# Recurrent layer and first attention: where the norm statistics, the low-rank product's mixing and the group root are computed

## The chip, the cores and the metric

The kernel runs on one core of a Trainium2 chip, in one launch. The metric is the device time in microseconds, the median of several runs.

## The reference

Input x is (16, 64, 256): 1024 rows of 256 channels, with a context of the same shape. Four layers follow one another: (0) self attention, cross attention (16 heads of 16) and an MLP; (1) an instance-normed attention with 64x64 weights; (2) two cross attentions with 16 heads of 128 and an MLP; (3) a recurrent layer with a channel MLP. The change touches layer 0's attentions and layer 3. Layer 3, cut to what matters:

```
xa = ln(x, ln1_w, ln1_b)
sx = concat([state[:, 1:2] - xa[:, :1], xa[:, :-1] - xa[:, 1:]], axis=1)
xxx = tanh((xa + sx * maa_x) @ maa_w1).reshape(b, l, 5, 32)
xxx = einsum('blfd,fde->blfe', xxx, maa_w2)
xm = xa[:, :, None] + sx[:, :, None] * (maa_stack + xxx)     # xk, xw, xv, xr, xg
w = exp(-exp(time_decay + tanh(xw @ td_w1) @ td_w2))
r, k, v, g = xr @ Wr.T, xk @ Wk.T, xv @ Wv.T, silu(xg @ Wg.T)
# scan over the 64 steps, 32 heads of 8: s = k v^T + w * s;  out = r (u * k v^T + s)
og = group_norm(out, groups of 8) * gn_w + gn_b
x1 = x + og * g @ Wo.T
xc = ln(x1, ln2_w, ln2_b); sx2 = shifted difference of xc
return x1 + sigmoid((xc + sx2 * ffn_maa_r) @ Wfr.T) * (relu((xc + sx2 * ffn_maa_k) @ Wfk.T) ** 2 @ Wfv.T)
```

## The kernel before

The 1024 rows are 8 tiles of 128 rows (two sequences of 64). Each engine has its program written out by hand, and semaphores join them: `done[name].did(i)` is raised by the step `name` of tile i, `done[name].at(i)` is waited for. Every engine executes its steps in the written order, so a step that waits holds up all behind it.

**First attention** (`attn0_*`). 16 items (self for tiles 0 to 7, cross for tiles 0 to 7, interleaved) run through 19 slots. A step called as `step(slot - 2)` works on the item that entered two slots earlier. VectorE (`attn0_vector`) computes per slot: the row statistics of a finished cross item (`row_stats`, `row_variance`: only in slots 9, 11 and 13 to 18), the mask product (`multiplied`, L590), its addition (`masked`, L596), `top`, the context (`context`, L614 and L618), `shifted` (L606), `stats` and `variance` of the next item (L538 to L548), `keys` (L572, which spreads the keys over a block diagonal, kdiag), and `add` (L626). TensorE's `scores` (L345) waits for kdiag. ScalarE evacuates, takes the exponential and makes the normed rows (`normed`, L204) from the scale that GpSimd computes (`rstd`, L196 and L198). GpSimd also adds the bias rows and splits the finished rows in a high and a low part (`row_split`, L219 and L221) for the MLP behind it; the MLP's first products and gelus (L811, L838) are begun in the last attention slot.

**Recurrent layer** (`rwkv_*`). The 8 tiles run through 16 slots of the same kind. TensorE's slot of tile i has `turn` (transposes), `lora` (the first low-rank product, into mx_ps), `mixes` (the second, L1871); one slot later `decay1`, `project` (r, k, v, g), `spread0`; two later `decay2`, `spread1`; three later `gather`, `center`, `turn_heads`, `attended`; four later `turn_ffn`; five later `ffn1`, `ffn2`. The transposed normed rows lie in `xa` with one column of state ahead of each sequence. The low-rank product of xa + sx * maa_x is taken without that sum: as xa (shifted by one column) times w1 - w1 * maa_x plus xa times w1 * maa_x, both weights prepared by GpSimd in `rwkv_consts_gpsimd` while layer 2 runs. That makes 12 matmuls, 24 TensorE instructions in 4-byte floats.

VectorE's slot holds `products0`, `bonus`, `out_heads`, `mix2` (L2211), `products1` (L2227), `group_sum` (L2278), `shift` (L2193, makes sx), the first three scans (`scan0`, L2246), `group_rstd` (L2284), `group_norm` (L2291), the other five scans (`scan1`, L2246), `ffn` (L2305), `receive` (L2262), `gate`, `attended` (L2297), `close` and `mix1` (L2203). ScalarE squares the centred heads, and `std` (L2082) takes the root of the group variance with the Sqrt function, whose table is another than that of the Tanh before and after it (L2111). GpSimd's slot holds the norm scales, copies of state columns, `receive` (L2391, the product rs0 over the first three scans), `gated` (L2398) and `bonus` (L2405). TensorE's `turn_ffn` of tile i waits for VectorE's `ffn` of tile i - 1.

Slots are counted by TensorE's below: in slot s it does `turn(s)`, the first scans of tile s - 2, the group norm of tile s - 3 and the ffn product of tile s - 5. Slot 3 is the first with a group norm, slot 5 the first with an ffn product.

Of the kernel before, what the change touches and what calls it, by code (L numbers as in the profile page):

```python
# [19 lines left out]
P = 128  # L20
# [247 lines left out]
def attn0_tensor(pe, ph, m):  # L268
# [139 lines left out]
    for slot in range(SLOTS):  # L408
# [12 lines left out]
        turn_rows(slot - 3)  # L421
# [6 lines left out]
def attn0_scalar(act, ph, m):  # L428
# [85 lines left out]
    for slot in range(SLOTS):  # L514
# [3 lines left out]
        rows(slot)  # L518
        if slot == SLOTS - 1:
            for u in range(STREAMS):  # L520
                gelu_rows(act, ph, m, ACT.Gelu_apprx_tanh, u, 0, 0)
        mlp_rows(slot - 3)
# [6 lines left out]
def attn0_vector(vec, m):  # L529
# [109 lines left out]
    for slot in range(SLOTS):  # L639
# [14 lines left out]
        if slot:  # L654
            stats(slot + 1)
            variance(slot + 1)
        keys(slot)
        if slot == 0:
            vec.wait_ge(m.s_x[1], 16)
            stats(1)  # L660
            variance(1)
# [3 lines left out]
def attn0_gpsimd(pool, ph, m):  # L665
# [34 lines left out]
    for slot in range(SLOTS + 1):  # L700
        if slot == 0:
            rstd(0)
        row_rstd(slot - 3)
        bias(slot)
        row_bias(slot - 4)
        row_split(slot - 4)
# [1104 lines left out]
def rwkv_consts_gpsimd(pool, m, before):  # L1811
# [5 lines left out]
    pool.tensor_tensor(m.maa_w1s, m.maa_w1[:, :, :], wide("maa_x", NX), ALU.mult)  # L1817
# [4 lines left out]
    pool.tensor_tensor(m.maa_w1[:, :, :], m.maa_w1[:, :, :], m.maa_w1s, ALU.subtract)  # L1822
# [4 lines left out]
def rwkv_tensor(pe, m, before):  # L1827
# [21 lines left out]
    def lora(i):  # L1849
        xa = m.xa[i % 2]  # L1850
        pe.wait_ge(*done["xa"].at(i))
        pe.wait_ge(*done["a_state"].at(i))
        if i >= 1:
            pe.wait_ge(*done["mixed"].at(i - 1))
        for n, width in enumerate((P, P, 2 * DM)):
            cols = slice(n * P, n * P + width)
            last = product(m.mx_ps[0:width, n * P:(n + 1) * P],
                           [(m.maa_w1[:, k, cols], xa[:, k, :, 1:S + 1]) for k in range(KD)]
                           + [(m.maa_w1s[:, k, cols], xa[:, k, :, 0:S]) for k in range(KD)])
# [154 lines left out]
def rwkv_scalar(act, m):  # L2014
# [64 lines left out]
    @of_tile  # L2079
    def std(i):  # L2080
        act.wait_ge(*done["gsum"].at(i))
        act.activation(m.sm[0][:, :], m.sm[0][:, :], ACT.Sqrt, bias=m.col("eps"), scale=1.0 / HS)\  # L2082
            .then_inc(*done["gstd"].did(i))

    @of_tile
# [47 lines left out]
    act.wait_ge(m.s_gn, 1)  # L2133
    a_normed(0)
    for slot in range(TILE_SLOTS):
# [5 lines left out]
        ffn_rows(slot - 5)  # L2141
        rows(slot)
# [3 lines left out]
        std(slot - 3)  # L2146
# [6 lines left out]
def rwkv_vector(vec, m, ph):  # L2153
    done = m.tile_done

    def stats(i, tag, at):
        a = i % 2
        vec.bn_stats(m.stats[a][:, at, :], m.x[:, i, :]).then_inc(*m.own_vec.did(tag + "_stats", i))

    def variance(i, tag, at):  # L2160
        a = i % 2
        vec.wait_ge(*m.own_vec.at(tag + "_stats", i))
        if i >= 2:
            vec.wait_ge(*done[tag + "_xn"].at(i - 2))
        vec.bn_aggr(m.mv[a][:, at, :], m.stats[a][:, at, :]).then_inc(*m.own_vec.did(tag + "_mv", i))
        vec.wait_ge(*m.own_vec.at(tag + "_mv", i))
        vec.tensor_scalar(m.rstd[a][:, at:at + 1], m.mv[a][:, at, 1:2], EPS, None, ALU.add)\
            .then_inc(*done[tag + "_eps"].did(i))

    @of_tile  # L2170
    def a_stats(i):
        vec.wait_ge(m.s_acc, 14 + 2 * (i // 4))
        stats(i, "a", 0)

    @of_tile
    def a_variance(i):
        variance(i, "a", 0)

    @of_tile
    def f_stats(i):  # L2180
        vec.wait_ge(*done["x1"].at(i))
        stats(i, "f", 1)

    @of_tile
    def f_variance(i):
        variance(i, "f", 1)

    @of_tile
    def shift(i):
# [4 lines left out]
            .then_inc(*m.own_vec.did("sx", i))  # L2194

# [625 lines left out]
```

## Time and profile before

| | us |
|---|---|
| median of 3 runs | 1036.51 |
| lowest, highest | 1035.86, 1045.05 |
| profiled execution, its own time | 1037.27 |
| its span | 1035.4 |
| TensorE busy | 946.3 (91%) |
| VectorE busy | 595.9 (58%) |
| ScalarE busy | 431.0 (42%) |
| GpSimd busy | 410.0 (40%) |
| first attention | about 0 to 165 |
| recurrent layer | about 838 to 1035.4 |

PE is TensorE's matmul queue, PEld its weight loads, DVE VectorE, ACT ScalarE, POOL GpSimd. A row of the timeline has the start, the duration, the engine, the source line, the operation, output and inputs with their shapes, how many instructions are merged, and in brackets how long the engine was idle before it and what ended that. A row of a table by line has the count, then busy us in all, mean ns of one, and the idle time before them.

### The profile page before, as it was taken

The numbers are of one execution on the slowest core, as the hardware profiler recorded it, in microseconds if no ns is written. First come the engines' busy times: TensorE is split into PE (matmuls) and PEld (weight loads), VectorE is DVE, ScalarE is ACT, GpSimd is POOL, SyncE is SP. The second block draws the span as 40 slices with busy tenths as digits, with TensorE's granted clock in tenths as the row PEclk, the third lists the DMA queues.
The fourth block names the chain that finished last, engine by engine and source line by source line (L and its number), as shares of the span: only waits on it lengthen the run. The fifth ranks groups of instructions, "written<-read, shape, count | busy, mean of one in ns | idle before, by whom it ended". The sixth has DMA issues, their size and how long they took to land.

```text
span 1035.4 us, 21403 instructions
## 1 busy us (share of the span) xinstructions
PE 946.3 (91%) x8296; PEld 803.9 (78%) x8296; DVE 595.9 (58%) x1004; ACT 431.0 (42%) x910; POOL 410.0 (40%) x558
## 2 busy tenths in 40 slices
PE   6888887968989999999999999999996978999986
PEld 4667765856778888899887988888985877878854
DVE  5889993667644443334363444433357457988871
ACT  3566663237643333333343333333323223545542
POOL 2223253875366343333166432433317512333320
PEclk9999997999999999999998999999998998999997
DMA  9000000140011110111101111110100100000000
GB/s 307 11 2 1 3 1 11 42 150 1 2 52 47 51 51 24 47 36 51 47 19 54 37 51 46 51 51 21 41 16 22 41 1 1 1 6 7 6 12 15
DMA packets 24145, 37.12 MB, mean 36 GB/s; under 512 B 4432, under 2 KB 16528, under 8 KB 23824
## 3 DMA queue, kind: packets, MB, share of 16 engines
q1 hardware_dynamic: 24080, 36.23, 11.3%
q8 instruction: 44, 0.72, 0.3%
q14 instruction: 21, 0.17, 0.1%
HBM read 35.17 MB, written 1.05 MB: 35 GB/s over the span
## 4 chain that ended last, share of the span: by engine, by line
PE 76%; DVE 8%; ACT 7%; issue 4%; POOL 4%; DMA 1%; SPq 0%; ACTq 0%; POOLq 0%; DVEq 0%
PE ps L1193 16%; PE ps L722 11%; PE ps L1832 9%; PE ps L1210 9%; PE ps L1252 6%; PE ps L1228 3%; PE ps L811 3%; PE ps L394 2%; PE ps L345 2%; PE ps L1238 2%; PE ps L1983 1%; PE ps L1910 1%; PE ps L297 1%; ACT sb L1617 1%; PE ps L1871 1%
## 5 line engine op out<-in xcount | busy, mean ns | idle before, releaser
L772 POOL TENSOR_TENSOR sb<-sb 128x256 fp32r<-128x256 f32 (+1 forms) x128 | 95.5, 746 | 302.0 <-DMA sb<-in_heads_a 149.7
L1193 PE MATMUL ps<-sb 128*128 128x512 f32 x768 | 187.8, 396 | 1.0 <-issue 1.0
L1193 PEld LDWEIGHTS ps<-sb 128*128 128x128 f32 x768 | 139.6, 188 | 33.0 <-ACT sb L1318 3.2
L722 PE MATMUL ps<-sb 128*128 128x256 f32 x1152 | 148.7, 287 | 0.5 <-DVE sb L859 0.4
L722 PEld LDWEIGHTS ps<-sb 128*128 128x128 f32 x1152 | 142.5, 193 | 2.7 <-issue 0.8
L774 POOL TENSOR_TENSOR sb<-sb 128x256 fp32r<-128x256 f32 (+1 forms) x128 | 115.6, 903 | 10.0
L1832 PE MATMUL ps<-sb 128*128 128x128 f32 (+2 forms) x672 | 101.0, 309 | 12.4 <-ACT sb L2116 6.3
L1832 PEld LDWEIGHTS ps<-sb 128*128 128x128 f32 (+1 forms) x672 | 89.6, 202 | 21.8 <-issue 8.0
L1415 DVE SCALAR_TENSOR_TENSOR sb<-ps,sb 128x512 fp32r<-128x512 f32 x64 | 45.1, 747 | 97.5 <-ACT sb L1351 97.5
L1210 PE MATMUL ps<-sb 128*128 128x256 f32 x768 | 99.2, 285 | 0.4 <-DVE sb L1383 0.4
L1210 PEld LDWEIGHTS ps<-sb 128*128 128x128 f32 x768 | 95.0, 191 | 3.0 <-issue 0.9
L1395 DVE TENSOR_REDUCE sb<-ps 128x8 f32<-128x520 f32 x32 | 22.4, 699 | 127.9 <-PE ps L1228 127.9
L1318 ACT ACTIVATE sb<-ps,sb 128x512 f32<-128x512 f32 x64 | 43.8, 685 | 109.2 <-PE ps L1193 109.2
L196 POOL TENSOR_TENSOR sb<-sb 128x1 f32<-128x1 f32 x40 | 22.0, 550 | 146.4 <-DVE sb L548 72.9
L1351 ACT ACTIVATE sb<-ps,sb 128x512 fp32r<-128x512 f32 x64 | 40.5, 684 | 82.3 <-PE ps L1252 82.3
L1252 PEld LDWEIGHTS ps<-sb 64*128 64x128 f32 x1024 | 61.3, 192 | 9.2 <-issue 5.1
L1252 PE MATMUL ps<-sb 64*128 64x64 f32 x1024 | 65.8, 280 | 1.6 <-ACT sb L1344 1.6
L1383 DVE TENSOR_TENSOR sb<-ps,sb 128x512 f32<-128x512 f32 x64 | 43.9, 690 | 37.4 <-PE ps L1210 37.1
L811 PE MATMUL ps<-sb 128*128 128x512 f32 x192 | 51.3, 427 | 8.1 <-POOL sb L774 4.6
L811 PEld LDWEIGHTS ps<-sb 128*128 128x128 f32 x192 | 39.0, 208 | 17.7 <-POOL sb L774 5.8
L1335 ACT ACTIVATE sb<-ps,sb 128x512 f32<-128x512 f32 x64 | 43.4, 679 | 15.7 <-PE ps L1193 15.5
L838 ACT ACTIVATE sb<-ps,sb 128x512 f32<-128x512 f32 x32 | 21.9, 689 | 66.3 <-PE ps L811 66.2
(211 smaller groups left out, 1595.7 us busy)
## 6 DMA issues: line engine op xcount, KB each, us to landing
sb<-in_heads_a SPq DMA_DIRECT2D x32, 386.0 KB, 3.0
sb<-in_heads_c SPq DMA_DIRECT2D x16, 256.0 KB, 3.6
sb<-in_heads_b SPq DMA_DIRECT2D x32, 128.0 KB, 2.9
sb<-in_mlp_a SPq DMA_DIRECT2D x16, 128.5 KB, 2.1
sb<-in_mlp_b SPq DMA_DIRECT2D x16, 128.0 KB, 2.1
sb<-in_w_r SPq DMA_DIRECT2D x1, 2048.0 KB, 7.6
sb<-in_encT SPq DMA_DIRECT2D x1, 1024.0 KB, 5.9
sb<-in_ctx SPq DMA_DIRECT2D x1, 1024.0 KB, 8.3
```

What stands on the lines that cost most here:

```text
L722: last = pe.matmul(m.acc(t), lhsT[x], rhs[w], start=opens and n == 0, stop=False, skip_group_check=True)
L772: pool.tensor_tensor(high, src, one, ALU.mult).then_inc(*G.did(name + "_high", u))
L774: pool.tensor_tensor(low, src, high.bitcast(F32), ALU.subtract).then_inc(*G.did(name, u))
L811: last = pe.matmul(m.ps[u][:, c, :], m.w_parts[u][w][:, k * P:(k + 1) * P], m.h_parts[x][:, k, c * 512:(c + 1) * 512], start=n == k == 0, ...
L1193: last = pe.matmul(m.ps[u][:, c, :], m.w_parts[u][w][:, (KD * q + k) * P:(KD * q + k + 1) * P], rows[x][:, k, c * 512:(c + 1) * 512], star ...
L1210: last = pe.matmul(m.ps[u0][:, c0, b * 2 * P:(b + 1) * 2 * P], m.enc_parts[x][:, k, (2 * j + b) * P:(2 * j + b + 1) * P], m.wv_parts[w][:, ...
L1252: last = pe.matmul(m.ps[1 - u][:, o, j * P + b * S:j * P + (b + 1) * S], m.v[j // 2][half, 2 * (j % 2) + b, u, :], m.pT[u][half, j, b * S: ...
L1318: act.activation(head_keys_of(m, u)[:, 8 * c:8 * c + 8, 0:S], m.ps[u][:, c, :].rearrange("p (n k) -> p n k", k=S), ACT.Identity, bias=m.he ...
L1335: act.activation(m.qT[u][:, c * 512:(c + 1) * 512], m.ps[u][:, c, :], ACT.Identity, bias=m.head_col(u, 0)).then_inc(*hd.qk.act.did(f"q{c}" ...
L1383: vec.tensor_tensor(dst, m.ps[u0][:, c0, :].rearrange("p (b c) -> p b c", b=2), bc(m.v_row[:, :], 1, [P, 2, 2 * P]), ALU.add).then_inc(*hd ...
L1415: vec.scalar_tensor_tensor(out=m.ctx_low(u, o), in0=m.ctx_ps(u, o), scalar=m.bv[u][:, :], in1=m.ctx_high(u, o).bitcast(F32), op0=ALU.add, ...
L1832: last = pe.matmul(out, lhsT, rhs, start=n == 0, stop=n == len(terms) - 1)
```

## The change

In the recurrent layer: (1) VectorE computes `xl` = xa + sx * maa_x in a new step `lora_rows` (two operations) behind `shift`, and TensorE's `lora` takes that alone, with half as many matmuls; the two scaled weights aren't prepared. (2) The statistics of both layer norms go from VectorE's bn_stats to ScalarE: a sum by Identity, the negated mean, a sum of squares by Square; GpSimd finishes variance, root and scaled mean. `a_rstd` moves one GpSimd slot on. (3) The group norm's root goes from ScalarE's Sqrt and VectorE's reciprocal to GpSimd, as power -0.5 over 128x32, in a new step `group_rstd` ahead of `receive`.

In the first attention: (4) VectorE's `stats` and `variance` of the next item come behind `keys`; GpSimd's `row_split` comes ahead of `row_rstd` and `bias`; in the last slot TensorE turns the last rows between the two first MLP products, and ScalarE evacuates them ahead of the gelus.

```diff
@@ -418,7 +418,10 @@
             for u, free in enumerate((done["qT"], done["pT1"])):
                 pe.wait_ge(*free.at(len(ITEMS) - 1))
                 fc1(pe, ph, m, 4, u, 0, 0)
-        turn_rows(slot - 3)
+                if u == 0:
+                    turn_rows(slot - 3)
+        if slot < SLOTS - 1:
+            turn_rows(slot - 3)
         keys(slot)
         turn_context(slot - 2)
         query(slot)
@@ -516,10 +519,10 @@
+        mlp_rows(slot - 3)
-        mlp_rows(slot - 3)
@@ -651,14 +654,11 @@
         top(slot - 1)
         context(slot - 2)
         shifted(slot - 1)
-        if slot:
-            stats(slot + 1)
-            variance(slot + 1)
         keys(slot)
         if slot == 0:
             vec.wait_ge(m.s_x[1], 16)
-            stats(1)
-            variance(1)
+        stats(slot + 1)
+        variance(slot + 1)
         add(slot - 2)
 
 
@@ -700,10 +700,10 @@
+        row_split(slot - 4)
-        row_split(slot - 4)
@@ -1814,12 +1814,10 @@
-    pool.tensor_tensor(m.maa_w1s, m.maa_w1[:, :, :], wide("maa_x", NX), ALU.mult)
-    pool.tensor_tensor(m.maa_w1[:, :, :], m.maa_w1[:, :, :], m.maa_w1s, ALU.subtract)
@@ -1847,16 +1845,13 @@
-        xa = m.xa[i % 2]
-        pe.wait_ge(*done["xa"].at(i))
-        pe.wait_ge(*done["a_state"].at(i))
+        pe.wait_ge(*m.own_vec.at("xl", i))
-                           [(m.maa_w1[:, k, cols], xa[:, k, :, 1:S + 1]) for k in range(KD)]
-                           + [(m.maa_w1s[:, k, cols], xa[:, k, :, 0:S]) for k in range(KD)])
+                           [(m.maa_w1[:, k, cols], m.xl[i % 2][:, k, :]) for k in range(KD)])
@@ -2077,12 +2072,6 @@
-    def std(i):
-        act.wait_ge(*done["gsum"].at(i))
-        act.activation(m.sm[0][:, :], m.sm[0][:, :], ACT.Sqrt, bias=m.col("eps"), scale=1.0 / HS)\
-            .then_inc(*done["gstd"].did(i))
-    @of_tile
@@ -2115,11 +2104,33 @@
+    def stats(i, tag, at, dst):
+        a, own = i % 2, m.own_act
+        total, squares, mean = m.mv[a][:, at, 0:1], m.mv[a][:, at, 1:2], m.rstd[a][:, at:at + 1]
+        if i >= 2:
+            act.wait_ge(*done[tag + "_turned"].at(i - 2))
+        act.activation(dst[a][:, :], m.x[:, i, :], ACT.Identity, accum_out=total).then_inc(*own.did(tag + "_sum", i))
+        act.wait_ge(*own.at(tag + "_sum", i))
+        act.activation(mean, total, ACT.Copy, scale=-1.0 / D).then_inc(*own.did(tag + "_mean", i))
+        act.wait_ge(*own.at(tag + "_mean", i))
+        act.activation(dst[a][:, :], m.x[:, i, :], ACT.Square, bias=mean, accum_out=squares)\
+            .then_inc(*done[tag + "_eps"].did(i))
+    @of_tile
+    def a_stats(i):
+        act.wait_ge(m.s_acc, 14 + 2 * (i // 4))
+        stats(i, "a", 0, m.xn)
+    @of_tile
+    def f_stats(i):
+        act.wait_ge(*done["x1"].at(i))
+        stats(i, "f", 1, m.xn_last)
-        if i >= 2:
-            act.wait_ge(*done[tag + "_turned"].at(i - 2))
@@ -2139,11 +2151,12 @@
         lora(slot - 1)
         decay1(slot - 2)
         ffn_rows(slot - 5)
+        f_stats(slot - 4)
+        a_stats(slot + 1)
         rows(slot)
         decay2(slot - 2)
         f_normed(slot - 4)
         square(slot - 3)
-        std(slot - 3)
         relu(slot - 5)
         receive(slot - 5)
         relu_square(slot - 5)
@@ -2152,38 +2165,6 @@
-    def stats(i, tag, at):
-        a = i % 2
-        vec.bn_stats(m.stats[a][:, at, :], m.x[:, i, :]).then_inc(*m.own_vec.did(tag + "_stats", i))
...
@@ -2192,6 +2173,18 @@
+    @of_tile
+    def lora_rows(i):
+        vec.wait_ge(*m.own_vec.at("sx", i))
+        if i >= 2:
+            vec.wait_ge(*done["lora"].at(i - 2))
+        for k in range(KD):
+            split = lambda x: x.rearrange("p (b s) -> p b s", b=2)
+            last = vec.scalar_tensor_tensor(out=split(m.xl[i % 2][:, k, :]), in0=split(m.sx[i % 2][:, k * P:(k + 1) * P]),
+                                            scalar=m.col("maa_x", k), in1=m.xa[i % 2][:, k, :, 1:S + 1], op0=ALU.mult,
+                                            op1=ALU.add)
+        last.then_inc(*m.own_vec.did("xl", i))
@@ -2275,19 +2268,16 @@
+        if i >= 1:
+            vec.wait_ge(*done["gstd"].at(i - 1))
-    @of_tile
-    def group_rstd(i):
-        vec.wait_ge(*done["gstd"].at(i))
-        vec.reciprocal(m.rc[0][:, :], m.sm[0][:, :]).then_inc(*m.own_vec.did("grstd", i))
-        vec.wait_ge(*m.own_vec.at("grstd", i))
+        vec.wait_ge(*done["gstd"].at(i))
@@ -2321,27 +2311,23 @@
-        f_variance(slot - 7)
+        lora_rows(slot - 3)
-        group_rstd(slot - 6)
-        a_stats(slot)
-        a_variance(slot)
-        f_stats(slot - 6)
@@ -2350,8 +2336,15 @@
+        a, own = i % 2, m.own_pool
+        var, squares, mean, scale = (m.mv[a][:, at, 0:1], m.mv[a][:, at, 1:2], m.rstd[a][:, at:at + 1],
+                                     m.rstd2[a][:, at:at + 1])
-        norm_scales(pool, m, i % 2, at, (tag + "_pow", i), done[tag + "_rstd"].did(i))
+        pool.tensor_scalar(var, squares, 1.0 / D, EPS, ALU.mult, ALU.add).then_inc(*own.did(tag + "_var", i))
+        pool.wait_ge(*own.at(tag + "_var", i))
+        pool.tensor_tensor(scale, var, m.col("pow"), ALU.pow).then_inc(*own.did(tag + "_pow", i))
+        pool.wait_ge(*own.at(tag + "_pow", i))
+        pool.tensor_tensor(mean, mean, scale, ALU.mult).then_inc(*done[tag + "_rstd"].did(i))
@@ -2383,6 +2376,18 @@
+    @of_tile
+    def group_rstd(i):
+        n = D // HS
+        pool.wait_ge(*done["gsum"].at(i))
+        pool.tensor_scalar(m.sm[0][:, :], m.sm[0][:, :], 1.0 / HS, EPS, ALU.mult, ALU.add)\
+            .then_inc(*m.own_pool.did("group_var", i))
+        pool.wait_ge(*m.own_pool.at("group_var", i))
+        if i >= 1:
+            pool.wait_ge(*done["normed"].at(i - 1))
+        pool.tensor_tensor(m.rc[0][:, :], m.sm[0][:, :], m.col("pow").to_broadcast([P, n]), ALU.pow)\
+            .then_inc(*done["gstd"].did(i))
@@ -2410,8 +2415,9 @@
     for slot in range(TILE_SLOTS):
         f_rstd(slot - 6)
         a_state(slot - 2)
-        a_rstd(slot)
+        a_rstd(slot - 1)
         first(slot - 4)
+        group_rstd(slot - 5)
         receive(slot - 4)
         f_state(slot - 6)
         gated(slot - 5)
@@ -2538,8 +2544,9 @@
+        m.xl = [scaled(at, P) for at in (KD * (2 * D + P), KD * (2 * D + 2 * P))]
```

## Rows read from the trace of the kernel before

**Rows 1.** windows, recurrent layer: length, busy us by engine, PEclk, DMA share

```profile
899.00:969.00 70.00, 70.00 (x598) 57.89 (x597) 61.12 (x97) 37.45 (x81) 26.42 (x30) 1.00 0.02 5
...
881.00:886.00 5.00, 5.00 (x32) 5.00 (x32) 4.97 (x9) 1.40 (x3) 1.81 (x1) 0.66 0.00 0
```

**Rows 2.** chain of waits, one full slot: start, us, what

```profile
942.12 3.67 PE ps L1832 x28
...
946.15 1.45 PE ps L1832 x8
```

**Rows 3.** timeline of VectorE, slot 6 from its mix1 to the next

```profile
929.09 1.49 DVE L2203 TENSOR_TENSOR sb<-ps,sb 128x1280 f32<-128x1280 f32 x1 [0.90 <-PE ps L1871]
...
935.22 0.42 DVE L2278 TENSOR_REDUCE sb<-sb 128x32 f32<-128x256 f32 x1
...
935.89 1.85 DVE L2246 TENSOR_TENSOR_SCAN sb<-sb 128x256 f32<-128x256 f32 x3
...
938.01 0.42 DVE L2291 TENSOR_TENSOR sb<-ps,sb 128x256 f32<-128x256 f32 x1
...
938.36 4.16 DVE L2246 TENSOR_TENSOR_SCAN sb<-sb 128x256 f32<-128x256 f32 x5
...
943.02 0.42 DVE L2305 SCALAR_TENSOR_TENSOR sb<-sb,ps 128x256 f32<-128x256 f32 x1 [0.51 <-PE ps L1832]
...
949.17 1.49 DVE L2203 TENSOR_TENSOR sb<-ps,sb 128x1280 f32<-128x1280 f32 x1 [0.90 <-PE ps L1871]
```

**Rows 4.** timeline, first attention, slots 12 and 11

```profile
104.90 1.23 DVE L590 TENSOR_TENSOR sb<-ps,sb 128x1024 f32<-128x1024 f32 x1
...
110.54 0.42 DVE L538 BATCH_NORM_STATS2 sb<-sb 128x6 f32<-128x256 f32 x1
...
112.80 1.09 PE L345 MATMUL ps<-sb 64*64 64x256 f32 x16 [0.72 <-issue]
...
113.95 1.23 DVE L590 TENSOR_TENSOR sb<-ps,sb 128x1024 f32<-128x1024 f32 x1 [0.92 <-PE ps L345]
```

**Rows 5.** groups by line, ScalarE

```profile
L2111 ACT ACT_TABLE_LOAD x6 | 7.7, 1283 | 0.1
...
L1617 ACT ACTIVATION_READ_ACCUMULATOR sb<-ps,sb 128x1 f32 x32 | 6.9, 217 | 0.0
```

**Rows 6.** groups by line, power on GpSimd by columns, VectorE's reciprocal

```profile
L196 POOL TENSOR_TENSOR sb<-sb 128x1 f32<-128x1 f32 x40 | 22.0, 550 | 146.4 <-DVE sb L548 72.9 <-DVE sb L2167 50.7 <-DVE sb L563 21.9
...
L962 POOL TENSOR_TENSOR sb<-sb 128x4 f32<-128x4 f32 x4 | 4.1, 1034 | 11.4 <-DVE sb L911 11.4
...
L1487 POOL TENSOR_TENSOR sb<-sb 128x8 f32<-128x8 f32 x1 | 1.7, 1655 | 0.0
...
L2284 DVE RECIPROCAL sb<-sb 128x32 f32<-128x32 f32 x8 | 2.6, 329 | 1.2 <-ACT sb L2082 1.2
```

**Rows 7.** timeline, GpSimd beside VectorE

```profile
236.63 1.22 POOL L1759 TENSOR_SCALAR sb<-sb 128x256 f32<-128x256 f32 x1
...
237.37 1.22 DVE L1693 TENSOR_TENSOR sb<-sb 128x1024 f32<-128x1024 f32 x1
...
901.72 4.63 DVE L2246 TENSOR_TENSOR_SCAN sb<-sb 128x256 f32<-128x256 f32 x5
...
937.82 1.81 POOL L2391 TENSOR_TENSOR sb<-sb 128x768 f32<-128x768 f32 x1 [3.23 <-DVE sb L2246]
...
938.36 1.83 DVE L2246 TENSOR_TENSOR_SCAN sb<-sb 128x256 f32<-128x256 f32 x1
```

**Rows 8.** timeline, mix1 of slots 3 and 4, ffn product of slot 9

```profile
892.45 1.49 DVE L2203 TENSOR_TENSOR sb<-ps,sb 128x1280 f32<-128x1280 f32 x1 [1.08 <-PE ps L1871]
...
909.41 1.47 DVE L2203 TENSOR_TENSOR sb<-ps,sb 128x1280 f32<-128x1280 f32 x1
...
998.23 0.42 DVE L2305 SCALAR_TENSOR_TENSOR sb<-sb,ps 128x256 f32<-128x256 f32 x1 [0.24 <-PE ps L1832]
```

**Rows 9.** timeline, TensorE at the first attention's end

```profile
172.67 5.49 PE L811 MATMUL ps<-sb 128*128 128x512 f32 x12 [3.46 <-POOL sb L221]
```

More of the change, by code:

```diff
@@ L2133, in rwkv_scalar @@
     act.wait_ge(m.s_gn, 1)
+    a_stats(0)
     a_normed(0)
@@ L2154, in rwkv_vector @@
     done = m.tile_done
-    def stats(i, tag, at):
-        a = i % 2
-        vec.bn_stats(m.stats[a][:, at, :], m.x[:, i, :]).then_inc(*m.own_vec.did(tag + "_stats", i))
[L2160 to L2168, printed above, removed]
-    @of_tile
[L2171 to L2186, printed above, removed]
     @of_tile
@@ L2277, in group_sum @@
         vec.wait_ge(*done["square"].at(i))
+        if i >= 1:
+            vec.wait_ge(*done["gstd"].at(i - 1))
         vec.tensor_reduce(m.sm[0][:, :], m.sq[:, :].rearrange("p (h j) -> p h j", j=HS), AX, ALU.add)\
             .then_inc(*done["gsum"].did(i))
-    @of_tile
-    def group_rstd(i):
-        vec.wait_ge(*done["gstd"].at(i))
-        vec.reciprocal(m.rc[0][:, :], m.sm[0][:, :]).then_inc(*m.own_vec.did("grstd", i))
     @of_tile
@@ L2540, in build @@
         scaled = lambda at, n: consts[:, at:at + KD * n].rearrange("p (k n) -> p k n", k=KD)
-        m.maa_w1s, m.wfks, m.wfrs, m.headsum_u = (
-            scaled(at, n) for at, n in ((0, NX), (KD * NX, D), (KD * (NX + D), D), (KD * (NX + 2 * D), P)))
+        m.wfks, m.wfrs, m.headsum_u = (
+            scaled(at, n) for at, n in ((0, D), (KD * D, D), (KD * 2 * D, P)))
+        m.xl = [scaled(at, P) for at in (KD * (2 * D + P), KD * (2 * D + 2 * P))]
         m.xa = [x[:, 0:4 * (S + 1)].rearrange("p (k b s) -> p k b s", k=KD, b=2) for x in m.wa]
```

## Prediction, made before the change was built

> **What bounds the kernel now.** I read the windows first. The recurrent layer takes the last 197 us of the span. In its middle TensorE is busy for all of 70 us at full clock, VectorE for 61 of them; in the filling before it the granted clock of one stretch of 5 us was 0.66 after gaps of nearly 1 us [rows 1]. Then the chain of waits of one full slot: it is TensorE instruction behind instruction, with no gap [rows 2], and the slot lasts 949.17 - 929.09 = 20.08 us [rows 3]. So in slots 5 to 7 TensorE's own order is the limit. VectorE is the next one: it waits only 0.90 us before mix1 and 0.51 before the ffn product [rows 3]. Before slot 5 and after slot 7 the chain goes to and fro between TensorE, VectorE and ScalarE. In the first attention TensorE stands 0.72 us ahead of the scores (the page has "issue", but kdiag ends just before it), and VectorE stands 0.92 us before the product with the mask in slots that have no row statistics, and not at all in those that have them [rows 4].
>
> **Part 1, the low-rank product.** TensorE's x28 is 24 instructions of the lora product and 4 twice as wide, so 3.67/32 = 0.115 us for a narrow one [rows 2]. Twelve of 24 go: 1.4 us in each of 8 slots. VectorE gets two products of 128x128 a slot; from the shortest neighbour rows I take 0.55 us together. They are issued before the first scans. TensorE's lora now waits for them, but comes 7 us after shift in a full slot, so that wait costs nothing there.
>
> **Part 2, statistics to ScalarE.** VectorE loses bn_stats, bn_aggr and one small operation (about 0.75 us) for f in each slot, and for a in slots up to 4. ScalarE gets an Identity and a Square over 256 columns, each with an accumulator read (217 ns, [rows 5]), and a one-column copy: I estimate 1.45 us with its waits, twice in a slot with both. Its idle time before the row evacuation is over 3.5 us in a full slot, so it is covered. If that cover were gone, turn and lora would come late by the rest. At the start it is not: the chain to the first normed row grows by about 0.9 us, a_stats(1) stands in front of the first row evacuation (0.85 us), VectorE's shift and product (1.05 us) come before a product that is 1.5 us shorter: +1.3 us. GpSimd's operations for the scale are all one column wide, 0.25 and 0.55 us each, and it has idle time for them.
>
> **Part 3, the root of the group norm on GpSimd.** This is the large term. Out go a Sqrt on ScalarE with two table loads of 1.28 us around it [rows 5] and a reciprocal of 0.33 us on VectorE. In comes a pow over 128x32 on GpSimd. The kernel has pow over 1, 4 and 8 columns: 550, 1034 and 1655 ns [rows 6]. That is 155 ns a column from 4 to 8, and 161 from 1 to 4. For 32 columns I get 1655 + 24 x 155 = 5.4 us. The lower bound is VectorE's whole operation on such a tile, 0.33 us [rows 6]; the value lies near the three rows of the same operation, which fall on a line. Behind it are queued on GpSimd the product rs0, gated and bonus; and on VectorE group_norm waits, with the second part of the scans (five of them), the ffn product, the receiving product and gate behind it.
>
> Times from the start of group_sum (935.22 in the slot shown): before, group_norm starts at 2.79 and the last scan ends at 7.30 [rows 3]. After: 0.42 for the sum, 0.1 for the semaphore, 0.3 for the variance, up to 0.3 that it waits behind shift, 0.1, 5.4 for the pow, 0.1: group_norm starts at 6.8. The first scan behind it is held up by GpSimd's rs0 product, as now: a scan of 0.66 takes 1.83 us while that product of 1.81 us runs [rows 3, 7]. It starts 0.05 us after the pow and holds that scan until 8.45, and the five scans end at 11.45. Now gated and bonus fall into the scans as well. Where gated fell there, the five took 4.63 and not 4.16 us [rows 7, 3], so 0.48 for each: 12.4, which is 5.1 us later than now.
>
> What that costs in a slot:
> - Slots 3 and 4 have no ffn; VectorE decides. Receive, gate, attended follow the scans, 2.0 us, and mix1 starts at 6.04 + 12.4 + 2.1 = 20.5 us after the mix1 before; slot 4 took 909.41 - 892.45 = 16.96 [rows 8]. That is +3.6, and in slot 3, with a little more slack and an easier start, +2.5.
> - Slots 5 to 7: the ffn product ends at 6.04 + 12.4 + 0.45 = 18.9, and turn_ffn, attended, decay1 and mixes need 3.4 more on TensorE: 22.3 against 20.08, and against 19.68 in slot 5: +2.6, +2.2, +2.2.
> - Slots 8 and 9: the ffn product starts when the scans end. It started at 998.23 in slot 9 [rows 8], with group_sum at 991.05; now 11.6 behind that: +4.4, and +4.7 in slot 8 the same way.
> - Slot 10 has no scans: turn_heads waits for the pow and delays the ffn product: +1.6.
> These are 23.8 us. What the shorter lora still gives is in the slots before a group norm exists: slots 1 and 2, 1.8 us each, since TensorE ran at half clock in a part of them; with +1.3 at the start the filling gives -2.3. In slots 3 to 7 the 1.4 us is counted already: TensorE just waits longer. Recurrent layer: +21.5.
>
> **Part 4, first attention.** kdiag moves 0.74 us up [rows 4], since the statistics start 0.74 before it. In the nine slots without row statistics the scores come 0.55 to 0.75 us earlier. Their cost: the normed row comes 1.3 us later, so GpSimd's bias addition now meets VectorE's masking (two tiles from SBUF) and holds it up by some 0.4. I take 0.3 for each, -2.7. In row slots VectorE has no gap, and order does not change its sum: 0. In the last slot, the rows are turned and evacuated ahead of the table load and both gelus, and GpSimd's split, for which TensorE waits 3.46 us [rows 9], comes 2 us earlier: -2. Moving row_split up uses idle GpSimd time: 0. Together -5 (between -2 and -8). The two products that leave the weights' preparation lie under a TensorE that is busy throughout: 0.
>
> **Sum.** +21.5 - 5 = +16.5. The profiled execution took 1037.3 us (span 1035.4); 1053.8 from there, and the median of the runs shown is 0.8 lower: **1053 us**.
>
> **A rule that would make it worse.** A scan that starts beside GpSimd's product waits for nearly all of it [rows 7]. But a VectorE product of two SBUF tiles that started at 237.37, beside a GpSimd operation with 0.48 us to go, took its usual 1.22 us [rows 7]: GpSimd holds VectorE only as long as it still reads, and reads well ahead. A pow of 32 columns is little to read and much to compute, so I count it as not holding the scans. The Trainium skill (SBUF — State Buffer, Who interferes with whom) says the opposite in the general case: whoever of GpSimd and a VectorE operation with two SBUF inputs comes first gets the shared ports for its whole instruction. The row at 237.37 speaks against that as far as it goes.
>
> **Rivals.**
> - *The pow holds the ports.* Then lora's second product and the first scans wait for the pow and run behind it: 1.75 us more in slots 3 to 7 and 1.2 in 8 and 9, +11: 1064. For it: every GpSimd product of 0.7 us and more has held up VectorE; against it the row just named. Chance 0.22.
> - *The pow is cheap*, on the other side: GpSimd's per-column price is a start-up that does not go on to 32 columns. It decides from about 1.7 us down: then the root is ready when the first scans and the two new products are done, and group_norm waits for nothing. Then slots 1 to 7 keep lora's gain where TensorE bounds them (1.8, 1.8, 1.6, 0.5, three times 1.4), the last slots lose 0.5 and one table load of 1.3 us [rows 5], less 1.3 at the start: -10.4, with -5 from the attention 1021. Three rows on a line speak against it. The Trainium skill (GPSIMD Engine Reference, Engine selection) has elementwise work at about twice VectorE's time; by it the root would take 0.7 us, an estimate. The rows at 4 and 8 columns are far above that already. Chance 0.10.
> - *Half way*: the pow costs 2.5 to 4 us, or gated and bonus don't meet the scans. Each us of pow is 7 to 8 us of time, so 1030 to 1046. Chance 0.15.
> - *TensorE's clock falls more.* TensorE now stands 2 to 4 us in each slot. After such gaps the granted clock fell to 0.66 for a stretch of 5 us [rows 1], so a part of it was at 1.2 and a part at 2.4 GHz, and 32 instructions took 5.44 and not 3.77 us. In most slots that stretch lies ahead of the wait for the ffn product and is hidden; if not, +1.7 us in six slots: 1063. In the upper part of the range, chance 0.05.
>
> **How the numbers follow.** The forecast's own case has 0.48, with 1046 to 1060 as its bounds (pow 4.7 to 5.6 us, 0 to 2 products in the scans, attention -2 to -8). The range that leaves out the cheap pow and the far end of the first rival is 1034 to 1067. About 1% is what can be told from no change, 1026 to 1047: faster 0.09, same 0.18, slower 0.73.
>
> **What would show it.** The group root's second GpSimd row over 128x32 at 5.4 us; a VectorE gap of some 3 us ahead of group_norm in each slot, released by GpSimd; the first scan of part two at 1.9 us, another one or two at 1.2; TensorE idle before turn_ffn; slots of 22.3 us from 5 to 7. In the attention the 0.7 us gap before the scores gone in slots without row statistics, and masking rows at 1.6 instead of 1.22. If the pow row is under 3 us or VectorE's scans of part one take over 6 us, I am wrong in the direction named.

## The result, and the profile after

The changed kernel takes 1064.4 us (median of 4 runs, 1060.2 to 1066.8) where the kernel before took 1037.9 in the runs beside it: ratio 1.024, 95% interval 1.018 to 1.030. In a second set of six runs it took 1066.7 us, ratio 1.024 again (1.021 to 1.028). It is slower, as forecast, and inside the range (1034 to 1067), but near its upper end: slower by 24 to 27 us where I had 16.5. The profiled execution took 1066.8 us, with a span of 1065.0.

First the timeline of VectorE, one full slot of the changed kernel, to be laid beside [rows 3]:

```profile
961.52 1.49 DVE L2196 TENSOR_TENSOR sb<-ps,sb 128x1280 f32<-128x1280 f32 x1 [1.89 <-PE ps L1866]
...
967.58 0.41 DVE L2273 TENSOR_REDUCE sb<-sb 128x32 f32<-128x256 f32 x1
...
968.88 1.85 DVE L2239 TENSOR_TENSOR_SCAN sb<-sb 128x256 f32<-128x256 f32 x3
974.03 0.42 DVE L2281 TENSOR_TENSOR sb<-ps,sb 128x256 f32<-128x256 f32 x1 [3.30 <-POOL sb L2389]
974.37 5.25 DVE L2239 TENSOR_TENSOR_SCAN sb<-sb 128x256 f32<-128x256 f32 x5
979.54 0.39 DVE L2295 SCALAR_TENSOR_TENSOR sb<-sb,ps 128x256 f32<-128x256 f32 x1
...
985.08 1.49 DVE L2196 TENSOR_TENSOR sb<-ps,sb 128x1280 f32<-128x1280 f32 x1 [2.20 <-PE ps L1866]
```

And GpSimd in the same slot:

```profile
968.08 0.32 POOL L2384 TENSOR_SCALAR sb<-sb 128x32 f32<-128x32 f32 x1 [4.43 <-DVE sb L2273]
968.48 5.52 POOL L2389 TENSOR_TENSOR sb<-sb 128x32 f32<-128x32 f32 x1
973.97 1.80 POOL L2396 TENSOR_TENSOR sb<-sb 128x768 f32<-128x768 f32 x1
...
976.27 1.16 POOL L2403 TENSOR_TENSOR sb<-sb 128x256 f32<-128x256 f32 x1
977.38 1.10 POOL L2410 TENSOR_TENSOR sb<-sb 128x256 f32<-128x256 f32 x1
```

Read from group_sum (967.58): group_norm starts at 6.45 us (before 2.79), the last scan ends at 12.04 (before 7.30), and the slot lasts 985.08 - 961.52 = 23.56 us (before 20.08). The power takes 5.52 us. The three scans that run beside it take 1.85 us, to the hundredth what they took without it; the five behind it, beside GpSimd's three products, take 5.25 and not 4.16.

Now TensorE in that slot, where this kernel stands; the last number in brackets is idle time and what ended it:

```profile
974.51 0.44 PE L1950 MATMUL ps<-sb 128*128 128x128 f32 x2 [0.17 <-DVE sb L2281]
974.78 2.50 PE L1830 MATMUL ps<-sb 128*128 128x256 f32 x16
980.07 0.41 PE L1964 MATMUL ps<-sb 128*128 128x128 f32 x2 [2.79 <-DVE sb L2295]
980.32 2.81 PE L1830 MATMUL ps<-sb 128*128 128x256 f32 x8
983.07 1.98 PE L1866 MATMUL ps<-sb 64*128 64x128 f32 x20
```

and the windows around it (length; busy us and instructions of PE, PEld, DVE, ACT, POOL; granted clock; DMA share and GB/s):

```profile
977.00:980.00 3.00, 0.28 (x3) 0.04 (x1) 3.00 (x5) 0.72 (x2) 1.49 (x2) 1.00 0.00 0
980.00:984.00 4.00, 3.93 (x20) 2.79 (x22) 2.42 (x4) 0.83 (x3) 0.00 (x0) 0.57 0.08 24
984.00:988.90 4.90, 4.90 (x54) 3.52 (x52) 3.65 (x5) 1.81 (x8) 1.11 (x4) 1.00 0.03 10
```

TensorE idles for 2.8 us, and when it goes on, the clock is at 0.57, mostly the lower of its two levels of 1.2 and 2.4 GHz, for the four microseconds in which the next mix1 is being made ready. The eight products of L1830 take 2.81 us, which took 1.45 in [rows 2]. Before, the clock of this layer's middle was 1.00 throughout [rows 1]; after, it is 0.91 in every 20 us from 929 to 989.

In the first attention the scores of slots 11 and 12 (TensorE, then VectorE's product with the mask):

```profile
99.69 1.09 PE L345 MATMUL ps<-sb 64*64 64x256 f32 x16 [0.21 <-issue]
108.76 1.09 PE L345 MATMUL ps<-sb 64*64 64x256 f32 x16 [0.21 <-issue]
```

```profile
101.47 1.22 DVE L593 TENSOR_TENSOR sb<-ps,sb 128x1024 f32<-128x1024 f32 x1
102.73 1.60 DVE L599 TENSOR_TENSOR sb<-sb 128x1024 f32<-128x1024 f32 x1
109.91 1.23 DVE L593 TENSOR_TENSOR sb<-ps,sb 128x1024 f32<-128x1024 f32 x1 [0.17 <-PE ps L345]
```

The gap ahead of the scores is 0.21 us and not 0.72 [rows 4], the masking takes 1.60. The scores of slot 12 stand at 108.76, 4.0 us ahead of 112.80. Yet the memset that opens the recurrent layer on VectorE starts at 834.10 us in this trace and at 834.20 in the one before. From these two traces alone the attention gained nothing and the layer lost 230.9 - 201.2 = 29.7 us. The runs below show which of the two can be trusted.

### The profile page after: what moved, and what is told of

The parts are those of the page before. It is cut to its first block, busy times and chain, and to the rows that moved or that the text cites. A ratio compares the mean times of both kernels' runs of the same rounds, so it can differ in the third digit from the quotient of the medians.

```text
span 1065.0 us, 21264 instructions
## 1 busy us (share of the span) xinstructions
PE 955.3 (90%) x8200; PEld 803.9 (75%) x8200; DVE 595.4 (56%) x964; ACT 428.3 (40%) x966; POOL 454.6 (43%) x588
## 4 chain that ended last, share of the span: by engine, by line
PE 61%; DVE 14%; POOL 10%; issue 8%; ACT 5%; DMA 1%; SPq 0%; DVEq 0%; ACTq 0%; POOLq 0%
PE ps L1193 16%; PE ps L722 11%; PE ps L1210 9%; PE ps L1252 6%; POOL sb L2389 4%; PE ps L1228 3%; PE ps L1830 3%; DVE sb L2239 3%; PE ps L811 3%; DVE sb L599 2%; PE ps L1238 2%; DVE sb L593 1%; PE ps L394 1%; ACT sb L1617 1%; PE ps L1521 1%
## 5 line engine op out<-in xcount | busy, mean ns | idle before, releaser
L772 POOL TENSOR_TENSOR sb<-sb 128x256 fp32r<-128x256 f32 (+1 forms) x128 | 98.2, 767 | 304.5 <-DMA sb<-in_heads_a 151.2
L722 PE MATMUL ps<-sb 128*128 128x256 f32 x1152 | 150.5, 289 | 0.4 <-DVE sb L859 0.4
L722 PEld LDWEIGHTS ps<-sb 128*128 128x128 f32 x1152 | 144.2, 196 | 2.4 <-issue 0.5
L774 POOL TENSOR_TENSOR sb<-sb 128x256 fp32r<-128x256 f32 (+1 forms) x128 | 115.5, 902 | 10.0
L1830 PE MATMUL ps<-sb 128*128 128x128 f32 (+2 forms) x576 | 96.8, 328 | 9.7 <-DVE sb L2220 3.3
L1830 PEld LDWEIGHTS ps<-sb 128*128 128x128 f32 (+1 forms) x576 | 82.3, 213 | 21.7 <-issue 9.8
L1318 ACT ACTIVATE sb<-ps,sb 128x512 f32<-128x512 f32 x64 | 43.8, 685 | 111.0 <-PE ps L1193 110.9
L2239 DVE TENSOR_TENSOR_SCAN sb<-sb 128x256 f32<-128x256 f32 x64 | 55.5, 929 | 0.0
L196 POOL TENSOR_TENSOR sb<-sb 128x1 f32<-128x1 f32 x24 | 13.2, 551 | 86.1 <-DVE sb L551 73.9
L1335 ACT ACTIVATE sb<-ps,sb 128x512 f32<-128x512 f32 x64 | 43.6, 681 | 15.7 <-PE ps L1193 15.6
```

Of the source, the lines that this page charges most:

```text
L722: last = pe.matmul(m.acc(t), lhsT[x], rhs[w], start=opens and n == 0, stop=False, skip_group_check=True)
L772: pool.tensor_tensor(high, src, one, ALU.mult).then_inc(*G.did(name + "_high", u))
L774: pool.tensor_tensor(low, src, high.bitcast(F32), ALU.subtract).then_inc(*G.did(name, u))
L1318: act.activation(head_keys_of(m, u)[:, 8 * c:8 * c + 8, 0:S], m.ps[u][:, c, :].rearrange("p (n k) -> p n k", k=S), ACT.Identity, bias=m.he ...
L1830: last = pe.matmul(out, lhsT, rhs, start=n == 0, stop=n == len(terms) - 1)
L2239: last = vec.tensor_tensor_scan(m.sc[:, j, :], m.wS[i % 2][:, :, :].rearrange("p n s -> p (n s)"), m.av[:, j, :, :].rearrange("p n s -> p ...
```

## The experiments

Each ratio is to the kernel before in runs on the same chip. Six to twelve runs of each stand against 11 to 29 of the kernel before, whose median there was 1040.3 to 1042.2 us: the 1035.4 us span shown ahead of the prediction lies low among its executions.

**The group root put back** (the changed kernel; root on ScalarE and VectorE in the old places):

```diff
@@ rwkv_scalar, rwkv_vector, rwkv_gpsimd
+        std(slot - 3)
...
+        group_rstd(slot - 6)
         group_norm(slot - 6)
...
-        group_rstd(slot - 5)
         receive(slot - 4)
```

> The changed kernel with the group root alone put back (Sqrt on ScalarE, reciprocal on VectorE, in their old places); the mixed rows, the statistics on ScalarE and the new order of the first attention stay. Theory, the root's 5.5 us on GpSimd is the whole loss: group_norm starts 2.8 us after group_sum again, a middle slot falls from 23.56 us to 20.09 less what the mixed rows save (1.4 less 0.55 of their own), some 19.2, and the time is 1020 to 1032 us. Rival, the statistics on ScalarE or the mixed rows cost something too, or the clock that the first attention loses is lost for good: slots stay at 20.1 us or above, and the time is 1037 us or more.

1030.9 us, ratio 0.990 (0.987 to 0.994). The loss is gone, and 1% is won. Middle slots last 18.8 us, 1.3 less than before; I had 19.2. The root is the whole loss: by the ratios (0.990 and 1.024) about 35 us lie between this kernel and the changed one.

**The first attention alone** (the kernel before with the attn0 functions of the changed one), in two sets of runs:

```diff
-        if slot:
-            stats(slot + 1)
-            variance(slot + 1)
         keys(slot)
         if slot == 0:
             vec.wait_ge(m.s_x[1], 16)
-            stats(1)
-            variance(1)
+        stats(slot + 1)
+        variance(slot + 1)
...
```

> The kernel before with the new order of the first attention alone. In the changed kernel's one trace the first attention was 5.9 us ahead at 205 us and nothing of that was left at 565 us, and three stretches at half clock lay between. Theory, TensorE's clock takes the lead back each time: the recurrent layer begins within 1 us of the kernel before, and the time is 1036 to 1039 us (ratio 0.998 to 1.002). Rival, that trace was one draw of the clock and the lead mostly stays: 1032 to 1034 us, ratio 0.994 to 0.997, as the prediction's term of 5 us has it.

1031.0 us, ratio 0.989 (0.986 to 0.993).

> The kernel before with the new first attention alone, again, as the measure beside the attention with mixed rows: ratio 0.986 to 0.993.

1032.4 us, ratio 0.992 (0.989 to 0.995). The lead stays, as the rival has it, and is even larger than the rival's 0.994 to 0.997. My theory, that the clock takes it back, had rested on one trace. The table shows why that misled. It has the start of the memset that opens the layer, the granted clock up to 829 us, and from the memset to the end:

| kernel | opens, us | clock to 829 | layer, us |
|---|---|---|---|
| before | 834.2 | 0.98 | 201.2 |
| root alone | 836.2 | 0.97 | 233.2 |
| mixed rows alone | 836.5 | 0.98 | 195.6 |
| statistics alone | 840.7 | 0.97 | 202.3 |
| changed | 834.1 | 0.97 | 230.9 |
| changed again | 829.7 | 0.97 | 231.0 |
| root put back | 829.4 | 0.98 | 199.4 |
| attention alone | 831.2 | 0.97 | 201.7 |
| attention again | 829.7 | 0.97 | 198.6 |
| attention and mixed rows | 831.0 | 0.97 | 199.4 |
| sixteen columns | 828.2 | 0.98 | 204.5 |
| filled | 831.4 | 0.97 | 258.1 |
| filled once | 830.4 | 0.98 | 230.4 |
| group_norm behind the scans | 829.3 | 0.97 | 211.4 |

The four kernels with the old attention open the layer at 836.9 us on average, the ten with the new one at 830.4: 6.5 us earlier. A single trace lay up to 4 us later than its group's average and up to 3 us earlier; the changed kernel's was the latest of the ten, and the one before the earliest of the four.

**The group root alone** (the kernel before; pow on GpSimd, as in the change):

```diff
-        std(slot - 3)
...
-        group_rstd(slot - 6)
         group_norm(slot - 6)
...
         first(slot - 4)
+        group_rstd(slot - 5)
```

> The kernel before with the group root alone on GpSimd, statistics and products as they were. Theory, the root costs more than the whole change loses, and the other parts gain: group_norm some 6.5 us after group_sum in place of 2.8, one us more in the scans beside the gated products, a stretch at half clock in each slot: 4.5 to 5.5 us a slot over eight slots and 1070 to 1080 us. Rival, the root costs what the traces differ by and the other parts nothing: 1060 to 1066 us. Second rival, without the other parts' early idle time the pow hides better: under 1055 us.

1070.2 us, ratio 1.028 (1.024 to 1.031): at the foot of the theory's span, and above the rival. The layer is 32.0 us longer. But its middle slots last 22.2 us, not 24.6 to 25.6, and the clock in them is whole. TensorE still computes the longer low-rank product there, and waits less for it (its timeline, and a window of 20 us, columns as above):

```profile
956.88 3.83 PE L1832 MATMUL ps<-sb 128*128 128x256 f32 x28
962.18 0.41 PE L1969 MATMUL ps<-sb 128*128 128x128 f32 x2 [1.47 <-DVE sb L2295]
962.43 1.61 PE L1832 MATMUL ps<-sb 128*128 128x256 f32 x8
```

```profile
949.00:969.00 20.00, 18.10 (x155) 14.61 (x155) 15.07 (x24) 5.69 (x16) 10.93 (x7) 1.00 0.02 8
```

So in the changed kernel, with 1.4 us less work for TensorE, a middle slot is 1.3 us longer: the work taken away became idle time ahead of the wait, and the half clock followed. The two kernels differ in the statistics too; the kernels filled with useless products, below, change TensorE's work alone.

**TensorE filled** (the changed kernel; the low-rank products computed four times, the last kept):

```diff
-        for n, width in enumerate((P, P, 2 * DM)):
...
+        for again in range(4):
+            for n, width in enumerate((P, P, 2 * DM)):
...
```

> The changed kernel in which TensorE computes the low-rank products four times over and keeps the last (some 2.2 us more work just ahead of the transposition that waits 2.8 us for the feed-forward rows). Theory, this idle time is what brings the stretch of 3.4 us at half clock in each slot: with it filled the clock stays at 1.00 from 885 to 1000 us, a slot falls from 23.56 to 22.3 us, and the time falls by 5 to 8 us against the changed kernel (1056 to 1060). Rival, the half clock comes from the wait at group_norm or has nothing to do with the idle time: the stretches stay and the time is 1063 to 1070 us.

1092.4 us, ratio 1.050 (1.047 to 1.054): a miss as an experiment on time. A pass took 1.45 us, twice what I had taken, so 4.4 us were added where 2.8 were free, and in the early slots none was. What it does show: with TensorE busy the clock was whole from 927 to 1025 us, and from turn_ffn to mix1 a slot took 3.46 us and not 5.01.

**Filled once**: one pass, for tiles 4 to 7 only.

```diff
-        for n, width in enumerate((P, P, 2 * DM)):
...
+        for again in range(2 if 4 <= i < 8 else 1):
+            for n, width in enumerate((P, P, 2 * DM)):
...
```

> The changed kernel in which TensorE computes the low-rank products of tiles 4 to 7 twice and keeps the second. The run with them four times over showed one pass to take 1.45 us (not the 0.7 us that I had taken), the clock whole from 926 to 1025 us, and mix1 3.46 us after the transposition in place of 5.01: the half clock costs 1.55 us of a slot, hidden there by 2.2 us too much filling. Theory: one pass fits into the 2.8 us, leaves the path alone and keeps the clock whole: 1.0 to 1.5 us a slot in four slots, 4 to 6 us less than the changed kernel. Rival, 1.3 us of idle time that are left still bring the half clock: nothing changes, within 2 us.

1062.6 us (ratio 1.020, 1.016 to 1.024), against 1066.7 for the changed kernel beside it (1.024, 1.021 to 1.028). The intervals overlap, so the total decides nothing. The trace does decide on the slot: TensorE in one, and the windows of three,

```profile
970.26 4.17 PE L1830 MATMUL ps<-sb 128*128 128x256 f32 x28
975.56 0.41 PE L1965 MATMUL ps<-sb 128*128 128x128 f32 x2 [1.12 <-DVE sb L2296]
975.80 1.61 PE L1830 MATMUL ps<-sb 128*128 128x256 f32 x8
```

```profile
929.00:949.00 20.00, 18.71 (x158) 14.74 (x158) 15.34 (x23) 8.66 (x28) 10.53 (x12) 1.00 0.02 7
949.00:969.00 20.00, 18.88 (x161) 14.86 (x160) 15.84 (x23) 7.73 (x23) 9.61 (x11) 1.00 0.03 9
969.00:989.00 20.00, 18.71 (x156) 14.59 (x155) 16.36 (x21) 7.55 (x22) 9.47 (x11) 1.00 0.02 8
```

for the changed kernel

```profile
929.00:949.00 20.00, 17.21 (x138) 13.06 (x137) 15.52 (x23) 9.02 (x28) 9.14 (x13) 0.91 0.02 7
949.00:969.00 20.00, 17.04 (x130) 13.19 (x131) 15.66 (x22) 7.29 (x21) 8.01 (x12) 0.91 0.02 8
969.00:989.00 20.00, 17.04 (x134) 13.12 (x132) 13.88 (x19) 6.21 (x19) 10.60 (x9) 0.91 0.02 7
```

With useless work the middle slots last 22.0 us in place of 23.6. From the first to the sixth group_sum it gains 3.9 us on the changed kernel's second trace. But the layer as a whole is 230.4 us long against 231.0. From the sixth group_sum to the end it took 1.9 us more than the kernel not filled, with a lower clock there (0.74 against 0.80 from 1000 to 1060 us), and up to the first group_sum 1.3 us more.

**Sixteen columns** (the changed kernel; the power is taken of 16 of 32 columns, the others get none, which leaves part of the computation out):

```diff
-        pool.tensor_tensor(m.rc[0][:, :], m.sm[0][:, :], m.col("pow").to_broadcast([P, n]), ALU.pow)\
+        some = m.rc[0][:, 0:16]
+        pool.tensor_tensor(some, some, m.col("pow").to_broadcast([P, 16]), ALU.pow)\
...
```

> The changed kernel with the power taken of 16 of the 32 columns alone (the other 16 groups are left undivided by their root). Theory, the power costs by the column (0.17 us each) and group_norm's wait is plain waiting: the power falls from 5.5 to 2.9 us, each of eight slots by 2.7 us or a little less where TensorE ends last, and the idle time of TensorE ahead of the transposition for the feed-forward falls from 2.8 us to nothing, so that the stretches at half clock go too: 20 to 27 us less, 1036 to 1043 us. Rival, the power has a large fixed price, or the scans and TensorE are the bound by themselves once 1 us is taken away: 1045 us or more.

1038.7 us, ratio 0.997 (0.995 to 1.000): 28 us less than the changed kernel beside it, just above the theory's 20 to 27. The power (groups by line: busy us, mean ns | idle before):

```profile
L2389 POOL TENSOR_TENSOR sb<-sb 128x16 f32<-128x16 f32 x8 | 24.3, 3032 | 0.7
```

In the changed kernel the same line has 5551 ns: 157 ns a column, 0.5 us besides. Middle slots last 18.8 us at full clock, group_norm waits 0.78. So in the middle slots a power of 3 us costs nothing against the root put back, which has 18.8 us too, and 2.5 us more cost 4.8 us in each. Behind them it does cost: slots 8 and 9 last 17.8 and 18.6 us, with the root put back 15.7 and 15.6, and the time is 0.997 and not 0.990.

Slot 8 (TensorE's slots, as ahead of the prediction) is also a second look at the clock. TensorE in the changed kernel,

```profile
1004.02 0.66 PE L1964 MATMUL ps<-sb 128*128 128x128 f32 x2 [4.26 <-DVE sb L2295]
1004.48 2.96 PE L1830 MATMUL ps<-sb 128*128 128x256 f32 x8
```

and with sixteen columns:

```profile
978.98 0.41 PE L1964 MATMUL ps<-sb 128*128 128x128 f32 x2 [2.90 <-DVE sb L2295]
979.23 1.61 PE L1830 MATMUL ps<-sb 128*128 128x256 f32 x8
```

After 4.26 us of idle time the same products run at a granted clock of 0.53 (1004 to 1008 us), after 2.90 us at 1.00 (979 to 983). The slot is 4.3 us longer: the ffn product comes 2.5 us later after group_sum, as the power does, and what follows it takes 1.7 us more. This gap of 2.90 us is as long as those of the changed kernel's middle slots (2.79), and no half clock followed it, so the length of the gap alone does not decide.

**group_norm behind the scans** (the changed kernel):

```diff
         scan0(slot - 5)
+        scan1(slot - 5)
         group_norm(slot - 6)
-        scan1(slot - 5)
         ffn(slot - 8)
```

> The changed kernel with group_norm moved behind the second part of the scans on VectorE, so that the power of 5.5 us runs beside the scans. Theory, the root then costs less: scans end 8.2 us after group_sum, group_norm at 8.2 in place of 6.45, the feed-forward's product 1.4 us behind it, so that ffn starts at 10.5 in place of 12.0: 0.5 to 1.5 us a slot over five slots and 2 us in each of slots 8 to 10, 4 to 10 us less than the changed kernel. Rival, TensorE waits for group_norm at the transposition of the heads in the order of its queue, and what is behind it moves by 1.8 us in each slot: 8 to 15 us more.

1044.3 us, ratio 1.004 (1.001 to 1.006): some 20 us less than the changed kernel, twice the most I had expected. VectorE in a slot:

```profile
937.15 0.41 DVE L2273 TENSOR_REDUCE sb<-sb 128x32 f32<-128x256 f32 x1
...
938.46 4.76 DVE L2239 TENSOR_TENSOR_SCAN sb<-sb 128x256 f32<-128x256 f32 x8
943.60 0.42 DVE L2281 TENSOR_TENSOR sb<-ps,sb 128x256 f32<-128x256 f32 x1 [0.38 <-POOL sb L2389]
945.43 0.42 DVE L2295 SCALAR_TENSOR_TENSOR sb<-sb,ps 128x256 f32<-128x256 f32 x1 [1.40 <-PE ps L1830]
```

and GpSimd beside it:

```profile
938.05 5.51 POOL L2389 TENSOR_TENSOR sb<-sb 128x32 f32<-128x32 f32 x1
943.54 1.80 POOL L2396 TENSOR_TENSOR sb<-sb 128x768 f32<-128x768 f32 x1
```

All eight scans run beside the power and take 4.76 us, 0.6 each; in the changed kernel they take 1.85 + 5.25 = 7.1. I had let the scans meet GpSimd's products as ever. The power itself kept those products away. group_norm comes at 6.45 us after group_sum, no later than with the wait ahead of the scans, ffn at 8.3 and not 12.0, and a slot lasts 19.1 us. The root still costs: against the kernel with the root put back (0.990) this one, which has the same other parts, is some 14 us longer, and the changed one 35.

**The mixed rows alone** and **the statistics alone** (the kernel before with part 1, or part 2):

```diff
...
+        lora_rows(slot - 3)
         scan0(slot - 5)
...
```

> The kernel before with the mixed rows for the low-rank products alone. Root put back and the first attention alone were 1030.9 and 1031.0 us, so that mixed rows and statistics together come to nothing. Theory: the mixed rows gain 1.3 us in each of the five middle slots, as the lead in the trace with the root put back grows, and the statistics lose it: 1033 to 1036 us where the kernel before is 1040.6, ratio 0.993 to 0.996. Rival, TensorE's products saved are given back as a lower clock where the layer fills: ratio 0.998 to 1.002.

1038.5 us, ratio 0.997 (0.995 to 0.999): between the theory (0.993 to 0.996) and the rival (0.998 to 1.002). Middle slots last 18.8 us, 1.3 less.

```diff
...
+        f_stats(slot - 4)
+        a_stats(slot + 1)
         rows(slot)
...
```

> The kernel before with the row statistics of the recurrent layer alone on ScalarE. The mixed rows alone are 0.997 and the new first attention alone 0.989, together 0.986, and with the statistics added 0.990. Theory, as the prediction had it: the statistics are covered in the full slots and cost 1.3 us at the start and the chain of f statistics ahead of each tile's feed-forward in the last slots: ratio 1.001 to 1.004 (1 to 4 us more). Rival, VectorE's freed 1.45 us a slot shows: 0.990 to 0.995.

1042.1 us, ratio 1.001 (0.998 to 1.004): no difference.

**The first attention with the mixed rows** (the kernel before with parts 4 and 1), what the runs had pointed to:

> The kernel before with the new first attention and the mixed rows, the statistics on VectorE and the group root on ScalarE: what the runs so far point to as the best. Theory, the two gains add: ratio 0.984 to 0.988, 1024 to 1029 us, below the 1031 of the first attention alone. Rival, the clock takes the one gain for the other: 0.989 or more.

1031.0 us, ratio 0.990 (0.985 to 0.995). The median is the rival's, but the interval holds most of the theory's 0.984 to 0.988 as well: this, the attention alone and the root put back can't be told apart. From the first mix1 to the last it takes 120.9 us, and the attention alone 124.3 and 125.3 in its two traces. Filling and emptying took 1.1 and 5.2 us more than in those two, at a clock of 0.91 from 834 to 1000 us where the attention alone had 0.95 and 0.94. That the clock takes the gain is not shown by traces that differ so much among themselves.

## Why the prediction was right, and where it was short

**The direction and its mechanism held.** The power on GpSimd is the loss, group_norm waits for it, and the scans and the ffn product are queued behind that wait. Power 5.4 us forecast, 5.55 measured; group_norm 6.8 us after group_sum, 6.45 measured; the five scans end at 12.4, 12.04 measured; the idle time ahead of group_norm 3 us, 3.3 measured; slots 3 and 4 +2.5 and +3.6, measured +2.5 and +3.2. The time, though, lies outside the 1046 to 1060 us of the forecast's own case; the wide range holds it because the first and fourth rival had been let in.

**The term that was too small is "slots 5 to 7: 22.3".** They last 23.4 to 23.6. The sum for the layer was +21.5 and 29.7 is measured: 3.6 us more in these three slots, 3.1 from there to the end, 1.8 up to slot 2, and 0.3 less in slots 3 and 4. In slots 5 to 7 the missing 1.3 us is TensorE's clock. Filled once, with the power as slow as ever, the slot lasts 22.0. The step that was wrong is in the fourth rival: "In most slots that stretch lies ahead of the wait for the ffn product and is hidden". It is not: the idle time is the wait for the ffn product itself, and the half clock comes after it, on the products that lead to mix1. That rival's price, 1.7 us a slot, was about right (1.55 from turn_ffn to mix1); its chance of 0.05 was low. The prediction had TensorE standing 2 to 4 us in each slot (2.8 measured), but not that the gap ends where the slot's last chain begins. And the row it leaned on for "after such gaps" had gaps of nearly 1 us in front of the clock of 0.66, as its own first paragraph says, not of 2 to 4.

**Slots 8 and 9, +4.7 and +4.4,** are the same step again. From one group_sum to the next they last 22.1 and 20.6 us, where the forecast makes 20.4 and 18.8. Up to the ffn product they are 4.9 and 4.7 us longer than before, nearly as forecast. Behind it come another 1.5 us in each, for which the forecast had nothing: there the granted clock is 0.53 in slot 8 (1004 to 1008 us) and 0.62 in slot 9 (1025 to 1034), and the sixteen columns, at 1.00 in slot 8, need 1.7 us less for that part.

**"In slots 3 to 7 the 1.4 us is counted already: TensorE just waits longer"** was the other side of it. Waiting longer was not free: with the longer product (root alone) the slot is 22.2 us.

**The first attention: -5 forecast, between -2 and -8.** 6.5 us between the averages of the openings, and 8 to 10 us less in the medians of the attention alone, which reaches a little past the bound. In the changed kernel's own profiled execution nothing of it was to be seen. The separate terms show as forecast (the gap ahead of the scores down to 0.21 us in slots without row statistics, masking at 1.6 us), with the one for the slots too small: the last scores stand 3.8 us earlier (144.72 and not 148.54) where the sum had 2.7, and the first products of the MLP's second layer (L722) 5.8 us earlier (172.13 and not 177.96), where the whole sum had 4.7. So the layer's +29.7 and the attention's -6.5 make 23, and 24 to 27 is measured.

**Parts 1 and 2.** The mixed rows save 1.3 us in a full slot where TensorE bounds it. For the statistics +1.3 us at the start was forecast. From the memset to the first mix1 seven traces with the statistics on ScalarE (the filled kernel left out) take 13.1 us on average, and the six without 10.6: about +2.5, and most of what the sum had too little up to slot 2. With the statistics alone the layer is 1.1 us longer, less than two traces of one kernel differ (201.7 and 198.6 for the attention alone).

**The first rival, the power holding the ports**, gave 1064, which is the number measured, by a mechanism that isn't there: three scans beside the power take 1.85 us with it and without, and eight take 4.76. Where a rival's sum meets the result, only the rows tell which mechanism it was. The Trainium skill (SBUF — State Buffer, SBUF: two separate sides) has whichever comes first, a GpSimd operation that reads SBUF or a VectorE operation with two SBUF inputs, hold the shared ports for its whole instruction. Here the scans do not wait for the power of 5.5 us, and they do stretch beside the 1.8 us product; the measurement decides for these shapes. Why the power does not hold them is not shown: that GpSimd "reads well ahead" was the prediction's reading of one row, and no run tests it.

**The second rival, the cheap power**, had its threshold too low for the middle slots: with 3.0 us, not 1.7, they last 18.8 us, as with the root put back. In slots 8 and 9 even 3.0 us cost 2.1 and 3.0 us.

What stays open: the parts alone (1.028, 0.989 to 0.992, 0.997, 1.001) multiply to 1.014 to 1.017, and the whole is 1.024. The half clock that the mixed rows bring under the power may be a part of it; it wasn't tried with the attention's order taken out. And what besides the length of the gap decides whether the clock falls is open.

## What to carry to other kernels

Before an operation moves to an idle engine, look at what is queued behind its consumer. Against the kernel with the root put back, the same 5.5 us cost about 35 us with five scans behind the wait and about 14 us with the wait behind the scans, though the result was no later. Work taken off TensorE where another engine sets the slot turns into idle time just ahead of its critical products, and they may then run at half the clock. And with traces that differ by 4 us among themselves, the place of a gain of 5 us is read from several of them.

## What the runs showed of the hardware that I had not expected

- GpSimd's power costs by the column, up to 32 columns: 550 ns for 1, 1034 for 4, 1655 for 8 [rows 6], 3032 for 16, 5551 for 32. VectorE's reciprocal of the 32 takes 329 ns [rows 6].
- While it runs, VectorE's scans are not disturbed (0.6 us each); beside GpSimd's products of 256 to 768 columns the five take 5.25 us.
- In each middle slot of the changed kernel TensorE's clock falls after 2.8 us of idle time and is back 3 to 4 us later. After 1.5 us (root alone) and 1.1 us (filled once) it did not fall. But it did not fall after 2.9 us in slot 8 of the kernel with sixteen columns either, and before the change it was 0.66 after 0.90 us, earlier in the layer [rows 1].
